# GNN layer in eight groups: distance factors laid out by VectorE blocks and memory instead of TensorE transposes

## What is computed

```python
h = jnp.maximum(_layernorm(x, axis=-1), 0.0)
# the layer, with x = h
x_conv = relu(bn(conv2(relu(bn(conv1(h))))) + h)      # conv2 has 17 taps over the nodes
s = x @ w_se.T + b_se                                 # 3 numbers for each node
sq = jnp.sum(s * s, axis=-1)
dist = sq[:, :, None] + sq[:, None, :] - 2.0 * jnp.einsum('bnd,bmd->bnm', s, s)
A = jnp.exp(-dist) * mask
msg = relu(x @ w_msg.T + b_msg)
x_nmp = jnp.einsum('bnm,bmd->bnd', A, msg)
x_in = jnp.concatenate([x_conv, x_nmp], axis=-1)
gi = x_in @ w_ih.T + b_ih ; gh = x @ w_hh.T + b_hh
r, z = sigmoid(gi_r + gh_r), sigmoid(gi_z + gh_z)
out = x + (1 - z) * tanh(gi_n + r * gh_n) + z * h
```

## Time and profile before

| | before |
|---|---|
| median of 3 runs | 289.75 us (289.58 to 289.75) |
| the profiled execution's own time | 289.65 us |
| its span, first to last instruction | 287.5 us |
| PE busy | 276.3 us, 96% |
| DVE busy | 249.8 us, 87% |
| ACT busy | 164.5 us, 57% |
| POOL (GpSimd) busy | 49.7 us, 17% |
| mean granted TensorE clock | 0.996 |

### The profile page before, as it was taken

How to read it: one execution, slowest core, us unless ns; L and a number is a source line. 1 busy time by engine, 2 the same in 40 slices (tenths; PEclk the granted TensorE clock), 3 DMA queues, 4 the chain that set the end, 5 groups by cost and what they waited for, 6 DMA issues and landing times.

```text
span 287.5 us, 5282 instructions
## 1 busy us (share of the span) xinstructions
PE 276.3 (96%) x1866; PEld 248.8 (87%) x1866; DVE 249.8 (87%) x565; ACT 164.5 (57%) x271; POOL 49.7 (17%) x110
## 2 busy tenths in 40 slices
PE   7799899999998999999999999999999999999993
PEld 5498886998887998899888998899988998899993
DVE  6998988988998889978998889979898887986565
ACT  3785468745665267555675266563674366561363
POOL 7400020810015002320025002230025000130000
PEclk9999999999999999999999999999999999999998
DMA  7900014534241402532041312523012120001002
GB/s 240 372 22 0 6 70 146 138 135 169 75 148 38 163 23 74 185 105 81 21 195 43 116 69 74 183 72 114 2 67 117 39 74 2 29 7 39 0 2 73
DMA packets 9437, 25.36 MB, mean 88 GB/s; under 512 B 2626, under 2 KB 3140, under 8 KB 8644
## 3 DMA queue, kind: packets, MB, share of 16 engines
q1 hardware_dynamic: 9264, 25.03, 25.0%
q10 hardware_dynamic: 148, 0.01, 0.0%
HBM read 20.79 MB, written 4.24 MB: 87 GB/s over the span
## 4 chain that ended last, share of the span: by engine, by line
PE 67%; DVE 17%; issue 7%; ACT 5%; POOL 2%; DMA 1%; DVEq 0%; ACTq 0%; POOLq 0%
PE ps L1190 20%; PE ps L1192 19%; PE ps L1191 19%; PE ps L1274 4%; PE ps L1240 3%; DVE stats L747 2%; DVE wt_lo L789 2%; ACT wt_hi L448 1%; POOL rstd L376 1%; PE ps L1251 1%; DMA xin<-x_first 1%; DVE aff L945 1%; DVE v_lo L870 1%; DVE y L890 1%; PE ps L1264 1%
## 5 line engine op out<-in xcount | busy, mean ns | idle before, releaser
L1190 PE MATMUL ps<-v_hi,wt_hi 128*128 128x256 f32 x320 | 92.6, 289 | 3.1 <-DVE y L909 1.5
L1192 PE MATMUL ps<-v_hi,wt_lo 128*128 128x256 f32 x320 | 90.1, 282 | 0.0
L1191 PE MATMUL ps<-v_lo,wt_hi 128*128 128x256 f32 x320 | 89.9, 281 | 0.0
L1190 PEld LDWEIGHTS ps<-v_hi,wt_hi 128*128 128x128 f32 x320 | 60.3, 188 | 5.1 <-DVE wt_lo L789 1.8
L1191 PEld LDWEIGHTS ps<-v_lo,wt_hi 128*128 128x128 f32 x320 | 60.3, 188 | 0.3
L1192 PEld LDWEIGHTS ps<-v_hi,wt_lo 128*128 128x128 f32 x320 | 60.2, 188 | 0.0
L382 POOL TENSOR_TENSOR scale<-vpe,neg_half 128x8 f32<-128x8 f32 x6 | 10.6, 1767 | 110.5 <-DVE scale L764 110.5
L1190 PE MATMUL ps<-h_hi,wt_hi 128*128 128x512 f32 (+1 forms) x67 | 26.3, 392 | 0.3 <-DVE h_lo L799 0.2
L1192 PE MATMUL ps<-h_hi,wt_lo 128*128 128x512 f32 (+1 forms) x67 | 25.8, 386 | 0.0
L1191 PE MATMUL ps<-h_lo,wt_hi 128*128 128x512 f32 (+1 forms) x67 | 25.7, 384 | 0.0
L600 ACT ACTIVATE gate<-ps,par 128x512 f32<-128x512 f32 x14 | 9.6, 687 | 20.6 <-PE ps L1192 20.6
(11 more groups left out here) (160 smaller groups left out, 613.2 us busy)
## 6 DMA issues: line engine op xcount, KB each, us to landing
w<-ln_rows SPq DMA_DIRECT2D x6, 1024.0 KB, 4.7
mask<-adj_t SPq DMA_DIRECT2D x8, 512.0 KB, 3.4
xt<-x_t SPq DMA_DIRECT2D x8, 512.0 KB, 3.3
out<-gate SPq DMA_DIRECT2D x15, 256.0 KB, 2.0
xin<-x_nm SPq DMA_DIRECT2D x6, 512.0 KB, 3.3
w<-w_conv SPq DMA_DIRECT2D x1, 576.0 KB, 6.4
gate<-w_gate SPq DMA_DIRECT2D x1, 576.0 KB, 7.4
xin<-x_first SPq DMA_DIRECT2D x2, 256.0 KB, 2.9
```

The lines of the kernel that those rows point to most:

```text
L1190: pe.matmul(dst, wt_hi[:, blk, :], hi, start=start, stop=False)
L1191: pe.matmul(dst, wt_hi[:, blk, :], lo, start=False, stop=False)
L1192: return pe.matmul(dst, wt_lo[:, blk, :], hi, start=False, stop=stop)
```

## The change

From the third group on (`g` of 2 and more, `g > BY_TRANSPOSE`):

- `factor_transposes` on PE and `factor_rows` on ACT are gone. DVE's new `turn(g)` waits for the slots and transposes 32x32 blocks within each set of 32 partitions into a new tile `turned` (256 columns of fp32). It stands in front of `update(g - 1, 1)`.
- SP's new `factor_loads(g)` writes `turned` to a 128 KB buffer in memory with four DMAs of 32 KB (one for each 32 partitions, in runs of 32 numbers), waits until they have landed, and reads `rows` back with two DMAs (128 and 112 partitions, two runs of 512 bytes each). It stands after the load of `x_t` and ahead of the output's second half. `distance` waits for the two loads.
- PE: `distance` moves from behind `sub_conv(g, 1)` to behind `sub_conv(g, 5)`; both gathers move together behind `sub_conv(g, 8)`, in the last group behind `sub_conv(g, 7)`.
- ACT: `exponent` moves behind `m_shared(g, 1)` and the two `h_high`, both `graphs_of` behind `m_shared(g, 2)`, both `n_high` to the end of this stretch.
- DVE: both `masked` move behind `join_y(g, 0, 1)` and the first `h_low`; both `n_low` behind the last `join_y`.

Groups 0 and 1 stay as they are.

```diff
+        turned = sb("turned", [P, GB, SLOT], F32R)
...
             sem("rg_ready"), sem("v_ready"), sem("cand_ready"), sem("diff_ready"), sem("sum_ready"),
             sem("zd_ready"), sem("out_ready"))
+        BY_TRANSPOSE = 1
         BY_MATMUL = 1
...
             engine.wait_ge(s_ready, 2 * g + 2)
-            upto(engine, rows_ps, g)
+            if g <= BY_TRANSPOSE + 1:
+                upto(engine, rows_ps, g)
+            else:
+                engine.wait_ge(turned_ready, g - 1 - BY_TRANSPOSE)
             left, right = slots[:, 0], slots[:, 1]
             def twice(a):
...
                     sp.wait_ge(hf_ready, NCH * g)
                 sp.dma_start(col_ln, ln_rows.unsqueeze(0).broadcast_to([P, 2, GW])).then_inc(col_landed, 16)
+            def factor_loads(g):
+                done = g - 1 - BY_TRANSPOSE
+                sp.wait_ge(turned_ready, done + 1)
+                upto(sp, rows_landed, 32 * done)
+                for i in range(4):
+                    ns = slice(32 * i, 32 * i + 32)
+                    sp.dma_start(slot_rows.rearrange("(i s) q n -> s q i n", s=SLOT)[:, :, :, ns],
+                                 turned[ns].bitcast(F32).rearrange("s (q i) n -> s q i n", q=2)).then_inc(turned_stored, 16)
+                sp.wait_ge(turned_stored, 64 * (done + 1))
+                sp.wait_ge(dist_ps, g)
+                sp.dma_start(rows[:, 0:4:2, :].bitcast(F32), slot_rows).then_inc(rows_landed, 16)
+                sp.dma_start(rows[0:P - KD, 1:4:2, :].bitcast(F32), slot_rows[KD:P]).then_inc(rows_landed, 16)
             sp.wait_ge(hn_ready, NCH)
             sp.wait_ge(hn_first, 2)
...
                     sp.wait_ge(sum_ready, NCH * g)
                     sp.dma_start(xts[(g + 2) % 3][:], x_t[g + 2]).then_inc(xt_landed[(g + 2) % 3], 16)
+                if g > BY_TRANSPOSE:
+                    factor_loads(g)
                 sp.wait_ge(out_ready, NCH * (g - 1) + 2)
                 sp.dma_start(out[g - 1, :, cols(1)], ob[1]).then_inc(out_stored[1], 16)
                 if g + 1 < NG:
...
                 ahead = g + 1 < NG
                 update_rows(g - 1, 1)
                 candidate(g - 1, 1)
-                if g == 1:
-                    m_shared(g, 0)
+                m_shared(g, 0)
+                if g <= BY_TRANSPOSE:
                     factor_rows(g)
+                    exponent(g)
+                    m_shared(g, 1)
+                    if ahead:
+                        h_high(g + 1, 0)
+                        h_high(g + 1, 1)
+                        graphs_of(g + 1, 0)
+                    n_high(g, 0, 5)
+                    if ahead:
+                        graphs_of(g + 1, 1)
+                    m_shared(g, 2)
+                    n_high(g, 1, 7)
                 else:
-                    factor_rows(g)
-                    m_shared(g, 0)
-                exponent(g)
-                m_shared(g, 1)
-                if ahead:
-                    h_high(g + 1, 0)
-                    h_high(g + 1, 1)
-                    graphs_of(g + 1, 0)
-                n_high(g, 0, 5)
-                if ahead:
-                    graphs_of(g + 1, 1)
-                m_shared(g, 2)
-                n_high(g, 1, 7)
+                    m_shared(g, 1)
+                    if ahead:
+                        h_high(g + 1, 0)
+                        h_high(g + 1, 1)
+                    exponent(g)
+                    m_shared(g, 2)
+                    if ahead:
+                        graphs_of(g + 1, 0)
+                        graphs_of(g + 1, 1)
+                    n_high(g, 0, 5)
+                    n_high(g, 1, 7)
                 ghn_rows(g, 0)
                 xc_high(g)
                 if ahead:
...
                 dve.wait_ge(rg_ready, NCH * g + c + 1)
                 dve.wait_ge(gin_ps, NCH * g + c + 1)
                 dve.tensor_tensor(gn[c][:], bank(5), gn[c][:], ALU.add).then_inc(v_ready, 1)
+            def turn(g):
+                done = g - 1 - BY_TRANSPOSE
+                dve.wait_ge(slots_ready, g + 1)
+                upto(dve, turned_stored, 64 * done)
+                dve.transpose(turned[:].bitcast(F32).rearrange("p b (k s) -> p b k s", k=2),
+                              slots[:, :, :, 0:KD].bitcast(F32).rearrange("p k b s -> p b k s")).then_inc(turned_ready, 1)
             def update(g, c):
...
                     add_h(g)
                     update(g - 1, 1)
                 else:
+                    turn(g)
                     update(g - 1, 1)
                     join_b(g, 0)
                     join_b(g, 1)
                     add_h(g)
-                masked(g, 0)
-                masked(g, 1)
+                if g <= BY_TRANSPOSE:
+                    masked(g, 0)
+                    masked(g, 1)
                 if ahead:
                     ln_apply(g + 1, 0)
                     ln_apply(g + 1, 1)
                 add_shared(g, 0)
                 join_y(g, 0, 0)
                 join_y(g, 0, 1)
-                n_low(g, 0, 5)
+                if g <= BY_TRANSPOSE:
+                    n_low(g, 0, 5)
                 if ahead:
                     h_low(g + 1, 0)
+                if g > BY_TRANSPOSE:
+                    masked(g, 0)
+                    masked(g, 1)
                 add_shared(g, 1)
-                n_low(g, 1, 7)
+                if g <= BY_TRANSPOSE:
+                    n_low(g, 1, 7)
                 join_y(g, 1, 0)
                 if ahead:
                     h_low(g + 1, 1)
                 join_y(g, 1, 1)
+                if g > BY_TRANSPOSE:
+                    n_low(g, 0, 5)
+                    n_low(g, 1, 7)
                 if g + 2 < NG:
                     ln_stats(g + 2)
                 xc_low(g, 0)
...
                 last.then_inc(rows_ps, 1)
             def distance(g):
-                pe.wait_ge(rows_ready, g + 1)
+                if g <= BY_TRANSPOSE:
+                    pe.wait_ge(rows_ready, g + 1)
+                else:
+                    pe.wait_ge(rows_landed, 32 * (g - BY_TRANSPOSE))
                 if g == 0:
                     pe.wait_ge(msg_ready, 2)
...
             for g in range(1, NG):
                 ahead = g + 1 < NG
                 sub_conv(g, 0)
-                if g > 1:
-                    factor_transposes(g)
                 sub_conv(g, 1)
-                if g > 1:
-                    distance(g)
                 sub_conv(g, 2)
-                if g == 1:
+                if g <= BY_TRANSPOSE:
                     factor_transposes(g)
                 sub_conv(g, 3)
-                if g == 1:
+                if g <= BY_TRANSPOSE:
                     distance(g)
                 sub_conv(g, 4)
                 sub_conv(g, 5)
-                gather(g, 0, 5)
+                if g <= BY_TRANSPOSE:
+                    gather(g, 0, 5)
+                else:
+                    distance(g)
                 sub_conv(g, 6)
-                gather(g, 1, 7)
+                if g <= BY_TRANSPOSE:
+                    gather(g, 1, 7)
                 sub_conv(g, 7)
+                if not ahead:
+                    gather(g, 0, 5)
+                    gather(g, 1, 7)
                 sub_conv(g, 8)
+                if ahead and g > BY_TRANSPOSE:
+                    gather(g, 0, 5)
+                    gather(g, 1, 7)
                 gates_h(g, 0, ahead)
                 if ahead:
                     conv1(g + 1, 0, 0)
...
+    slot_rows = nc.dram_tensor("slot_rows", (P, 2, P), F32, kind="Internal").ap()
```

More of the change, by code:

```diff
@@ L58, with gnn_kernel @@
 NPAR = 14
-def gnn_kernel(nc, x_first, x_nm, x_t, adj_t, w_in, w_conv, w_gate, par_in, row_in, bias_in, ln_rows, out):
+def gnn_kernel(nc, x_first, x_nm, x_t, adj_t, w_in, w_conv, w_gate, par_in, row_in, bias_in, ln_rows, slot_rows, out):
     ctx = ExitStack()
@@ L177, in gnn_kernel @@
             sem("rows_ready"))
+        turned_ready, turned_stored, rows_landed = sem("turned_ready"), sem("turned_stored"), sem("rows_landed")
         dist_ps, e_ready, a_ready, nmp_ps, n_hi_ready, n_lo_ready = (
@@ L1510 @@
     ln_rows = nc.dram_tensor("ln_rows", (2, GW), F32, kind="Internal").ap()
-    gnn_kernel(nc, *args, ln_rows, out)
+    slot_rows = nc.dram_tensor("slot_rows", (P, 2, P), F32, kind="Internal").ap()
+    gnn_kernel(nc, *args, ln_rows, slot_rows, out)
     got = run_bass_kernel_spmd(nc, [arrays], core_ids=[0]).results[0]["out"]
```

## The result

The changed kernel takes 297.44 us (median of 6 executions, 296.23 to 298.94), the kernel before 289.58 us beside it (289.56 to 289.75). The ratio is 1.027, interval 1.024 to 1.030: it is slower by 7.9 us. I had forecast 289.0 us, range 285.8 to 292.2. The profiled execution of the changed kernel took 296.92 us and has a span of 295.0 us against 287.5. All ratios here leave out executions more than 1.5% above the fastest of the same kernel (two in experiment 3, one in experiment 8).

A forecast was written before the change was run, and what follows sets the result against it. The prediction took PE, busy 96% of the span, to bound the kernel. Its terms, -4.19 us of PE time and waits of 1.20 + 3 x 0.78, gave -0.65 us: from 289.65 to 289.0 us, range 285.8 to 292.2.

The forecast's parts named there:

- g = 2: PE's wait ahead of `distance` in this group, where PE arrives 0.77 us earlier against DVE and SP: 1.20 us.
- g = 3 to 5: PE's wait ahead of `distance` in each of these groups: rows there at 10.70 us, PE at 9.92, so 0.78 us.
- PE, removed: PE's saving: 0.57 us in each of six groups, 3.42 us, plus the 0.77 us slot wait; 4.19 us in all.
- DVE, added, and the moved steps: DVE's transpose, 0.43 us, fits the gap ahead of `update`; moved steps cause no PE wait, but shift DVE 0.35 us.
- The trip, its first half: From issue of the load of `x_t` to the stores' landing: 3.3 us for the load plus 0.81 for the stores.
- The trip, its second half: From the first read's issue to PE: 1.45 us landing without packets, 0.99 for the reads, 0.05 for PE.
- The rule of ring order: On SP's queue each DMA engine consumes descriptors in order, so the stores' packets begin when the `x_t` load's end.
- g = 6 and 7: No load of `x_t` in these groups; the trip ends 8.5 us after the turn's start at about 2.2 (2.55), no wait.
- C: Rival: longer trip, for instance 24 ns per store packet, trip 7.4 us, slower at 292.3 us; chance 0.27.
- Its second form: Alternative mechanism in C: the stores' four-dimensional issue takes twice the 0.45 us and no longer hides behind the load.
- B: Rival: stores don't wait for the load's packets, trip 5.7 us, only g = 2 waits, 0.3 us; 285.8 us; chance 0.22.
- D: Rival: an engine becomes the bound, transpose over 0.72 us or `n_low` after `conv1`'s turn; 290.2 us; chance 0.08.

The follow-up runs named there:

- experiment 3: Changed kernel with `factor_loads` ahead of the wait for `sum_ready` and of the load of `x_t`; 289.3 us, 289.0 without the two above 291, ratio 0.998.
- experiment 8: Changed kernel with `distance` one block later, behind `sub_conv(g, 6)`, except in the last group; 292.62 us, ratio 1.010.
- run 1: Changed kernel with reads landing in an unused tile, `distance` using the rows of g = 1 without waiting (wrong distances, for time alone); 285.65 us, ratio 0.986.
- run 2: Changed kernel's new places, but with the old transposes on PE and ACT's copy, without turn, stores and reads; 288.55 us, ratio 0.996.
- run 5: Changed kernel with ACT issuing two of the four stores, reads and places unchanged; 295.62 us, ratio 1.020.
- run 6: Changed kernel with `factor_loads` behind `sum_ready` but ahead of the load of `x_t`, which is issued only when the rows have landed; 296.15 us, ratio 1.023.
- run 4: Changed kernel with `factor_loads` ahead of the load of `x_t`, that load issued only when the rows have landed; 286.9 us, ratio 0.991.
- run 10: Changed kernel with `factor_loads` early, ACT issuing two stores and the second read: 285.68 us; with 1 KB pieces and the load held back too: 285.62 us.

## Why the prediction was wrong

The kind of loss was the one forecast, waits of PE for the rows, and so were the groups in which it acts, but nearly every term of the trip was too small, and one cost, the clock behind a wait, was not in the sum at all. The profiled execution, 7.3 us above the kernel before, is made up of 3.9 us of gain (run 1), 9.3 us of waits, 1.5 us of clock and 0.15 us in g = 6; 0.3 us are left over. The median is 0.5 us higher; how much of that is clock is not shown, but the slowest execution (298.94 us) also has the lowest mean clock, 0.981. Against the forecast's sum the largest misses are g = 2 (3.0 us), g = 3 to 5 together (2.7 us) and the clock (1.5 us).

- **PE, removed.** Predicted -4.19 us, measured -3.9. The transposes are nearly right, 0.44 us each time (run 1 against run 2) instead of 0.48. The 0.09 us for gathers in a row is wrong, it is 0.03: the pair takes 1.70 us (109.08 to 110.78) where I took twice 0.81. What I counted as gained stands inside the pair.
- **DVE, added, and the moved steps.** Predicted nothing; run 1 and 2 show nothing. The transpose took 0.45 us, the value taken was 0.43. The shift of DVE was 0.27 us (130.64 - 126.62 against 3.75) instead of 0.35.
- **The trip, its first half.** Predicted 4.11 us from the issue of the load to the stores' landing, measured 4.38 in g = 3. The rule of ring order agrees with run 5, where two stores landed after 3.7 to 4.15 us behind the load and after 2.92 without it (the Trainium skill, "DMA: Bandwidth & Descriptors", "Queues, rings and completion order"). But I put the stores' issue at 0.45 us from the earlier trace rows and called it hidden. It is 0.65 us each, and alone it gives the same 3.9 us, so taking away the queue brought 0.15 to 0.35 us only (run 6).
- **The trip, its second half.** This is the step that failed in g = 3 to 5. Predicted 2.5 us from the first read's issue to PE (1.45 + 0.99 + 0.05), measured 138.35 - 135.02 = 3.3. The sum had no term for the time in which the first read's issue holds up the second, 0.61 us, and from its own issue the second read took 2.7 us, not 2.5. The base of 1.6 us came from a write of 8 KB; for reads in short pieces I had no row. With both halves, PE waited 1.68 us where 0.78 was predicted.
- **g = 2.** Predicted 1.20 us, measured 4.22. This is the largest miss. From the load's issue to the stores' landing it took 99.29 - 93.16 = 6.1 us where the same 4.11 was predicted, and the second half took 3.5 us instead of 2.5. The stores landed 5.75 us after their first issue, not 3.95; in the seven kernels that issued all four on SP at about 93.4 us this was 4.8 to 5.75. Issued at 91.5 (runs 3 and 4) they took 4.0, and shared with ACT 3.8. The load of `x_t` is not the cause (run 6). A transfer of instructions on one DMA engine goes with it in every trace (behind run 6); that it is the cause is not shown.
- **The clock** has no term in the prediction at all. The waits were to be 0.8 to 1.2 us, and behind waits of that length the clock did not fall in any trace. They came out at 1.62 to 4.22 us, and the clock fell behind the longest, for 1.5 us; in other kernels such a fall cost 1.5 to 2.95 us.
- **g = 6 and 7.** No wait was predicted. It is right for 7; in g = 6 PE comes to `distance` 10.18 us after the group's start against 10.03 in g = 7, so some 0.15 us are lost. The second read's issue took 1.25 us there, beside a transfer of instructions.
- **The rivals.** C had the direction and the right place, a longer trip, but put it on the stores, at 292.3 us. Its second form, that the stores' issue no longer hides behind the load, came nearest: at 0.65 us each the four issues land the stores as late as the load does. B's trip of 5.7 us with its 285.8 us needed what run 10 built: an earlier start and two issuing engines. D did not occur.

## What to carry to other kernels

When a step of PE is replaced by a trip through memory, list the trip's start, each DMA's issue, its landing and the next issue, and take each price from a row of the same direction and piece size; if the sum comes near the time that PE needs to get there, do not count it as hidden; landings of one kernel's DMA lay up to 1.8 us apart here. Put the trip's start ahead of every wait and every large load on its queue, keep large loads from behind its last read too, and let a second engine issue half. A wait of PE costs its length, and behind it perhaps a stretch at half clock.

## What the runs showed of the hardware

- The clock fell to 1.2 GHz behind waits of PE of 1.51 and 1.64 us in one execution, and didn't behind waits of 1.62 to 1.71 us in another, nor behind 2.04 us in a third. A fall cost 1.5 us of convolution in five cases, 2.6 us in two and 2.95 us in one.
- The issue of a DMA on SP took 0.33 us for 128 pieces of 1 KB, 0.57 us for 256 of 512 bytes, 0.61 us (0.65 from one to the next) for 256 of 128 bytes through four dimensions, and 0.38 us for 256 of 32 bytes. The same issue took longer right behind others: the output's second half 0.34 us by itself, 0.59 behind the two reads in 512 byte pieces, 0.43 behind those in 1 KB pieces. Single ones took 1.06 to 1.83 us, each ending 0.37 to 0.43 us after a transfer of 16 KB of instructions.
- Such a transfer took 0.9 to 2.3 us on one DMA engine. In run 6 the last packets of the stores came only when it had ended, 0.76 us behind the others.
- With a load of 512 KB issued right behind two reads on the same queue, the second read landed after 3.9 us in g = 3 and 5 (run 3); with the load held back it took 3.3 us at most (run 4).
- Executions of the kernels in which PE never waits for DMA lie 0.2 to 0.9 us apart (runs 1 and 10), those of the changed kernel 2.7 us.
